# First attention of batches 0 and 1: the reciprocals of the row sums move from VectorE to PoolE, as a power of minus one

## The chip, the cores and the metric

The kernel runs on one core of a Trainium2 chip. The metric is the device time of one execution in microseconds (us). A core has five engines, each of which takes its own instructions in the order in which they were written: TensorE (PE, matmuls and transposes), VectorE (DVE), ScalarE (ACT), PoolE (POOL, the GpSimd engine) and SyncE (SP, which here issues DMAs). Engines wait for each other through semaphores.

## The reference

Two transformer layers over x of shape (8, 1024, 256). What the change touches is the first attention, done for each of the 8 batches:

```python
def _L0_attn_ref(x, Mq, Mk, Mv):
    q = (x @ Mq).reshape(B, H, C, K)          # B=8, H=8, C=1024, K=64
    k = (x @ Mk).reshape(B, H, C, K)
    v = (x @ Mv).reshape(B, H, C, V)          # V=32
    scores = jnp.einsum('bhqk,bhck->bhqc', q, k).reshape(B * H, C, C)
    att = jax.nn.softmax(scores / jnp.sqrt(jnp.float32(K)), axis=1)
    out = jnp.einsum('bqhc,bhcd->bqhd', att.reshape(B, C, H, C), v)
    return out.reshape(B, C, H * V)
x = x + _L0_attn_ref(_layernorm(x), Mq, Mk, Mv)
x = x + _L0_ffn_ref(_layernorm(x), ...)       # weights and rows quantised to FP4 blocks
x = x + _L1_attn_ref(_layernorm(x), ...)      # 16 heads of 16, q and k normalised
x = x + _L1_ffn_ref(_layernorm(x), ...)       # top 2 of 8 low-rank experts
```

The kernel divides by the softmax's row sum not in the 1024 x 1024 matrix of weights but in the rows of v that those weights multiply.

## The kernel before

The batches run through a pipeline written out by hand. Each stage of a batch is a lane: a generator for each engine that yields a place before each piece of work. The function `weave` merges an engine's lanes by these places (table `PLACES`), so an engine's order is fixed when the kernel is built and nothing moves at run time. While batch b is in its second attention and experts, batch b + 1 is in its first attention. At the start this overlap is missing: beside the first attention of batch 0 runs only the preparation of the weights (quantising them to FP4: lanes `prep` and `prep_weights`), then comes the first half of batch 0's FFN input alone, and the first attention of batch 1 runs beside the FFN of batch 0 and then beside the head normalisation of batch 0's second attention (`heads`, `heads_norm`).

The first attention of a batch has 64 steps n, each of 128 query rows against 1024 keys (step n is head group n // 8, block n % 8). A step is a chain over four engines:

- PE, `attn0`: scores of the step into one of two halves of PSUM tile `pS` (line 761), which it may write when the exponential of step n - 2 has read it (wait on `e0_in`).
- DVE, `attn0`: the negative row maximum (`nmaxa`, line 1635).
- ACT, `attn0`: exp into one of four buffers (`EA[n % 4]`, line 1274, three of them parts of region `ua`), with the row sum into a column of `zz`; it signals `e0_in`. It may write a buffer when the values of step n - 4 have been multiplied (`pv0_in`).
- DVE, `sums0`: the reciprocal of that column, 128x1, into `rz` (line 1644), signal `rz_in`.
- POOL, `attn0`: 256 columns of v times the reciprocal into one of four buffers `vs` (line 2160, also a part of `ua`), signal `vs_in`; the profile puts its wait on line 2159.
- PE, `values0`: vs times the exponentials, into PSUM tile `pV` (line 886). PE's lane puts the values of step n - 3 behind the scores of step n. After 8 steps ACT (in batches 0 and 1) copies `pV` to `oTa` and PE transposes it.

Beside this, DVE, ACT and POOL work on the other lanes. Those that matter below: POOL's `prep_weights` (lines 2350, 2353, 2356, 2358, 2366, in turns with DVE's `prep`, lines 2012 to 2026), POOL's part of the FFN's quantisation in batch 0 (lines 2204, 2206, 2211, 2212, between DVE's lines 1562 and 1572), and POOL's `heads` and `heads_norm` (lines 2258, 2266, 2276 to 2300). POOL already uses the power elsewhere: four lanes take (variance + eps) to the power -0.5 of 2, 4 or 8 columns (lines 2136, 2146, 2182, 2328), with the exponent in a 128x1 tile `half` that a memset has filled.

The two pieces that the change is about are these:

```python
c = n % 8                                                      # DVE, sums0
e.wait_ge(e0_in, 64 * b + n + 1)
e.reciprocal(rz[:, c:c + 1], zz[:, c:c + 1]).then_inc(rz_in, 1)

e.wait_ge(rz_in, 64 * b + m + 1)                               # POOL, attn0
e.tensor_tensor(vs[m % 4], vv[:, :, 32 * c:32 * c + 32],
                rz[:, c:c + 1].unsqueeze(2).to_broadcast([128, 8, 32]), ALU.mult).then_inc(vs_in, 1)
```

Of the kernel before, what the change touches and what calls it, by code (L numbers as in the profile page):

```python
# [7 lines left out]
F32 = mybir.dt.float32  # L8
# [3 lines left out]
ALU = mybir.AluOpType  # L12
# [338 lines left out]
def timed(engine):  # L351

    def of(lane):

        def at(*args):
            keys = [(engine, lane.__name__, *args[:n]) for n in range(len(args), -1, -1)]
            places = next((PLACES[k] for k in keys if k in PLACES), ())
            for _, place in zip(lane(*args), places, strict=True):
                yield place
        return at  # L360
    return of
# [14 lines left out]
def build(nc, a, out):  # L376
    with ExitStack() as ctx:

        def sb(name, shape, dt=F32):
            return ctx.enter_context(nc.sbuf_tensor(name, shape, dt))  # L380

        def sem(name):
            return ctx.enter_context(nc.semaphore(name))
# [89 lines left out]
        tqw = [ub(2816 * i, [FI]) for i in range(8)]  # L473
        scw = [[ub(48 * K + 512 * i + 176 * n, [44]) for n in range(2)] for i in range(2)]
        amw = sb("amw", [128, 44])
        raw = {"mq": ub(24 * K, [2, 512]), "mk": ub(28 * K, [2, 512]), "mv": ub(32 * K, [2, 256])}
        xhb = sb("xhb", [128, NT * D])
        xhb_flat = xhb[:, :]
# [23 lines left out]
        zz = sb("zz", [128, 8])  # L502
        rz = sb("rz", [128, 8])
# [23 lines left out]
        s0_in, max0_in, e0_in, rz_in, vs_in, pv0_in = (sem(n) for n in ("s0", "max0", "e0", "rz", "vs", "pv0"))  # L527
# [79 lines left out]
        def job_to(n, k, w):  # L607
            _, n0, rn, _, s_ = jobs[n]
            return wd[0:w, :, k, n0:n0 + 128] if s_ is None else wgu[:, :, k, s_, n0:n0 + rn]
# [128 lines left out]
        def _(e):  # L738
# [430 lines left out]
            @timed("PE")  # L1169
            def prep():  # L1170
                for n, (_, _, rn, cols, _) in enumerate(jobs):
                    yield
                    e.wait_ge(wq_in, 5 * n + 5)
                    for c0 in range(0, cols, 128):
                        w = min(128, cols - c0)
                        u = take(("w", n, c0))
                        i = transpose(bank(u)[0:w, 0:rn], tqw[4 * (n % 2) + 1][0:rn, c0:c0 + w])
                        if w < 128:
                            i = e.matmul(bank(u)[w:2 * w, 0:rn], tqw[4 * (n % 2) + 1][0:rn, c0:c0 + w], ident[0:rn, 0:rn])
                        i.then_inc(r_full[u.bank], 1)  # L1180
                yield
                for o in range(2):
                    e.wait_ge(wrow[o], 16 * 8)
                    for k in range(2):
                        u = take(("W", o, k))
                        transpose(bank(u)[:, 0:128], tqw[4 * o][:, k * 128:k * 128 + 128]).then_inc(r_full[u.bank], 1)
                yield
                e.wait_ge(raw1_in, 16 * 13)
                for k in range(2):
                    u = take(("A", k))  # L1190
                    transpose(bank(u)[:, 0:128], small[:, k * 128:k * 128 + 128])
                    transpose(bank(u)[:, 128:136], small[0:8, 256 + k * 128:384 + k * 128]).then_inc(r_full[u.bank], 1)
                yield
                e.wait_ge(wrow[0], 16 * (8 + 16))
                for o in range(2):
                    u = take(("B", o))
                    transpose(bank(u)[:, 0:128], tqw[0][:, 256 * o:256 * o + 128]).then_inc(r_full[u.bank], 1)
# [14 lines left out]
        def _(e):  # L1212
# [243 lines left out]
            @timed("ACT")  # L1456
            def prep():
                for n, (_, _, rn, cols, _) in enumerate(jobs):
                    yield
                    for c0 in range(0, cols, 128):  # L1460
                        high(("w", n, c0), job_to(n, c0 // 128, 128)[:, 0, :], WS, lambda v: v[:, 0:rn])
                yield
                for o in range(2):
                    for k in range(2):
                        high(("W", o, k), wmoe[:, 0, k, 128 * o:128 * o + 128], WS, lambda v: v[:, 0:128])
                yield
                for k in range(2):
                    u = full(("A", k))
                    e.activation(wmoe[:, 0, k, 264:392], bank(u)[:, 0:128], ACT.Copy, scale=WS)
                    e.activation(wmoe[:, 0, k, 256:264], bank(u)[:, 128:136], ACT.Copy, scale=WS).then_inc(r_mid[u.bank], 1)  # L1470
                yield
                for o in range(2):
                    high(("B", o), bt[:, 0, o * 128:(o + 1) * 128], WS, lambda v: v[:, 0:128])
# [22 lines left out]
        def _(e):  # L1496
# [141 lines left out]
            @timed("DVE")  # L1638
            def sums0(b):
                for n in range(64):  # L1640
                    yield
                    c = n % 8
                    e.wait_ge(e0_in, 64 * b + n + 1)
                    e.reciprocal(rz[:, c:c + 1], zz[:, c:c + 1]).then_inc(rz_in, 1)  # L1644

            @timed("DVE")
            def outputs0(b):
# [456 lines left out]
            def lanes_y(i):  # L2104
                return [*([first(i + 1, attn0), first(i + 1, sums0), first(i + 1, outputs0), first(i + 1, projections)] if within(i + 1) else []),
                        *([placed(-6, prep()), placed(-6, prep_low()), prep_heads()] if i < 0 else []),
                        *([v for lane in (moe_x3, moe_gate, moe_M) for v in second(i - 1, lane)] if within(i - 1) else []),
                        *([heads(i), heads_bias(i), heads_norm(i)] if within(i) and i + 1 < NB else
                          [heads_end(), heads_bias(i), heads_norm_end(), heads_by_end(), heads_low_end()] if i + 1 == NB else [])]
# [5 lines left out]
        def _(e):  # L2115
# [3 lines left out]
            e.affine_select(out=ident[:, :], in_=ident[:, :], compare_op=ALU.not_equal, fill=1.0, base=0,  # L2119
                            pattern=[[-1, 128]], channel_multiplier=1).then_inc(const_in, 1)  # L2120
            e.memset(halfp[:, :], 0.5).then_inc(const_in, 1)
            for n in range(8):
                e.memset(iota[:, n:n + 1], float(n)).then_inc(const_in, 1)
            e.memset(vaug[:, :, :, 16:17], 1.0 / AS).then_inc(const_in, 1)
# [23 lines left out]
            @timed("POOL")  # L2148
            def attn0(b):

                for m in range(64):
                    yield
                    c = m % 8
                    if m > 3:
                        e.wait_ge(pv0_in, 64 * b + m - 3)
                    if m == 0:
                        u = ring["v0", b, 3]
                        e.wait_ge(r_free[u.bank], u.n)
                    e.wait_ge(rz_in, 64 * b + m + 1)
                    e.tensor_tensor(vs[m % 4], vv[:, :, 32 * c:32 * c + 32], rz[:, c:c + 1].unsqueeze(2).to_broadcast([128, 8, 32]), ALU.mult).then_inc(vs_in, 1)  # L2160

# [216 lines left out]
            def lanes_y(i):  # L2378
                return [*([first(i + 1, attn0)] if within(i + 1) else []), *([placed(-6, prep()), placed(-6, prep_weights())] if i < 0 else []), *([v for lane in (moe_rstd, moe_low, moe) for v in second(i - 1, lane)] if within(i - 1) else []),
                        *([spread("H", i), heads(i), heads_norm(i)] if within(i) and i + 1 < NB else  # L2380
                          [spread("H", i), heads_end()] if i + 1 == NB else [])]
# [349 lines left out]
```

## Time and profile before

| | |
|---|---|
| median of 3 runs | 2743.35 us (2740.52 to 2746.29) |
| the profiled execution, its own time | 2740.36 us |
| its span in the profile | 2738.6 us |
| busy share of the span | PE 93%, DVE 74%, ACT 73%, POOL 44% |
| chain that ended last, by engine | PE 47%, DVE 20%, ACT 9%, DMA 8%, POOL 6%, issue 6%, SP's queue 4% |
| first attention of batch 0 | 37 to 211 us |
| first attention of batch 1 | 259 to 470 us |

The page gives averages over the whole span. The first 470 us, which the change touches, look different from the rest: the pipeline is filling, and the busy share of PE is lower there. So the views below are taken by stretches. The 1.8 us between the span and the execution's own time lie around the profiled instructions and are not touched.

### The profile page before, as it was taken

To read this page: it belongs to the slowest core of one execution; us is meant where nothing else is said; L and a number is where in the kernel's file an instruction comes from. 1 tells how busy PE (TensorE), PEld (TensorE's weight loads), DVE (VectorE), ACT (ScalarE), POOL (GpSimd) and SP (SyncE) were. 2 spreads that over 40 slices of the span, in tenths; PEclk is the share of its full clock that TensorE was granted. 3 is DMA by queue.
4 is the path that set the end of the run, shared out by engine and by line. 5 is a ranking of instruction groups with operands and counts; after the bars stand their busy time and mean duration, and the time that the engine had idled before them with its cause. 6 is when DMAs were issued, how large, how long until landed. Compare 5 with 4: busy or idle time off the path is not lost.

```text
span 2738.6 us, 115342 instructions
## 1 busy us (share of the span) xinstructions
PE 2550.1 (93%) x50126; PEld 1409.9 (51%) x50126; DVE 2033.8 (74%) x4228; ACT 1990.4 (73%) x3791; POOL 1213.8 (44%) x1744
## 2 busy tenths in 40 slices
PE   7776877999999999999999999999999999999898
PEld 4445644445644566445654466445664457443434
DVE  6778866957888589866888589875888678865534
ACT  4552556886778867887778867887778867787785
POOL 5564475216733268124752167223762267411210
PEclk9998999999999999999999999999999999999999
DMA  5214332325423362324423243324532254232310
GB/s 134 45 36 89 53 68 73 73 36 103 104 53 82 56 122 73 76 51 85 109 72 77 51 98 92 81 48 66 114 93 66 42 97 96 57 72 44 95 26 24
DMA packets 458145, 200.66 MB, mean 73 GB/s; under 512 B 270110, under 2 KB 447622, under 8 KB 457614
## 3 DMA queue, kind: packets, MB, share of 16 engines
q1 hardware_dynamic: 455982, 192.15, 33.0%
q8 instruction: 412, 6.75, 1.0%
q10 hardware_dynamic: 1632, 0.79, 0.2%
q14 instruction: 119, 0.97, 0.1%
HBM read 46.48 MB, written 32.51 MB: 29 GB/s over the span
## 4 chain that ended last, share of the span: by engine, by line
PE 47%; DVE 20%; ACT 9%; DMA 8%; POOL 6%; issue 6%; SPq 4%; ACTq 0%; DVEq 0%; POOLq 0%
PE pR L761 18%; PE pV L1025 11%; PE pS L984 7%; DVE nmaxa L1635 6%; ACT ub L1332 6%; PE pS L761 5%; PE pV L886 3%; PE pR L771 2%; DMA xT<-ua 2%; SPq L2633 2%; DMA ua<-EA 1%; POOL ua L2160 1%; DMA ua<-ua 1%; DMA xT<-xhb 1%; POOL ub L2300 1%
## 5 line engine op out<-in xcount | busy, mean ns | idle before, releaser
L1332 ACT ACTIVATE ub<-pS 128x512 f32<-128x512 f32 x2048 | 1048.7, 609 | 162.5 <-PE pS L984 160.6
L1635 DVE TENSOR_REDUCE nmaxa<-pS 128x1 f32<-128x1024 f32 x512 | 621.0, 1216 | 150.9 <-PE pS L761 148.7
L1274 ACT ACTIVATE ua<-pS,nmaxa 128x1024 f32<-128x1024 f32 x384 | 427.9, 1115 | 246.4 <-DVE nmaxa L1635 241.1
L761 PE MATMUL pS<-ua 128*32 128x512 f16 x8192 | 542.9, 386 | 61.4 <-ACT ua L1274 33.8
L1025 PE MATMUL pV<-ub,vaug 128*17 128x512 f32 x4096 | 537.7, 597 | 0.0
L2160 POOL TENSOR_TENSOR ua<-ua,rz 128x256 f32<-128x256 f32 x512 | 330.6, 659 | 284.7 <-DVE rz L1644 278.1
L984 PE MATMUL pS<-ub 50*128 50x512 f16 x1920 | 339.0, 383 | 8.6 <-ACT ub L1332 1.6
L761 PEld LDWEIGHTS pS<-ua 128*32 128x32 f16 x8192 | 209.0, 98 | 225.4 <-ACT ua L1274 54.2
L761 PE MATMUL pR<-wgu,xT 128*32 128x352 f16 x6144 | 283.2, 317 | 26.4 <-DVE ub L1701 14.1
L984 PEld LDWEIGHTS pS<-ub 50*128 50x128 f16 x1920 | 94.5, 93 | 365.3 <-ACT ub L1332 314.5
L886 PE MATMUL pV<-ua 128*32 128x128 f32 x6144 | 241.2, 278 | 29.5 <-POOL ua L2160 27.0
L761 PEld LDWEIGHTS pR<-wgu,xT 128*32 128x32 f16 x6144 | 158.8, 97 | 168.4 <-issue 107.8
L886 PEld LDWEIGHTS pV<-ua 128*32 128x32 f32 x6144 | 167.7, 111 | 99.4 <-POOL ua L2160 50.4
L1274 ACT ACTIVATE EA<-pS,nmaxa 128x1024 f32<-128x1024 f32 x128 | 142.6, 1114 | 76.2 <-DVE nmaxa L1635 75.5
L2211 POOL TENSOR_TENSOR EA<-ua,EA 128x64 f16<-128x64 f32 x28 | 8.6, 307 | 394.7 <-DVE EA L1753 394.7
L761 PE MATMUL pR<-wqkv,xT 128*32 128x512 f16 (+1 forms) x3072 | 146.0, 327 | 4.2 <-DMA xT<-xhb 1.5
L1025 PEld LDWEIGHTS pV<-ub,vaug 128*17 128x17 f32 x4096 | 88.1, 96 | 91.8 <-issue 71.3
L761 PE MATMUL pR<-wd,ua 128*32 128x256 f16 x3808 | 128.3, 273 | 5.7 <-DMA ua<-EA 5.6
L761 PEld LDWEIGHTS pR<-wd,ua 128*32 128x32 f16 x3808 | 97.0, 96 | 65.3 <-issue 63.9
L1223 ACT ACTIVATE ua<-pR 128x512 f16<-128x512 f32 x128 | 75.8, 601 | 69.8 <-PE pR L761 51.2
L2211 POOL TENSOR_TENSOR ua<-ua 128x64 f16<-128x64 f32 x28 | 8.7, 309 | 235.3 <-DVE ua L1753 235.3
L761 PEld LDWEIGHTS pR<-wqkv,xT 128*32 128x32 f16 x3072 | 83.4, 97 | 53.2 <-issue 3.4
(274 smaller groups left out, 4081.2 us busy)
## 6 DMA issues: line engine op xcount, KB each, us to landing
ua<-ua SPq DMA_DIRECT2D x378, 128.0 KB, 2.8
ub<-scr SPq DMA_DIRECT2D x264, 64.0 KB, 2.7
scr<-ub SPq DMA_DIRECT2D x30, 512.0 KB, 4.2
x<-in_L_attn_x SPq DMA_DIRECT2D x32, 256.0 KB, 4.0
between<-x SPq DMA_DIRECT2D x28, 256.0 KB, 3.3
ub<-between SPq DMA_DIRECT2D x28, 256.0 KB, 3.8
out<-ub SPq DMA_DIRECT2D x28, 256.0 KB, 3.4
ub<-scr SPq DMA_DIRECT2D x192, 32.0 KB, 1.8
```

Source lines behind the costliest of these rows:

```text
L761: i = e.matmul(dst[j:j + 32], w[:, j:j + 32], m, start=start, stop=stop)
L771: return e.matmul(dst, src, ident[0:n, 0:n], is_transpose=True)
L886: i = e.matmul(pV[32 * jl:32 * jl + 32, 128 * jg:128 * jg + 128], vs[n % 4][:, j, :], EA[n % 4][:, 128 * j:128 * j + 128], start=(c == 0 a ...
L984: e.matmul(pS[:, 512 * hl:512 * hl + 512], kk_[row:row + 50, o, 128 * c:128 * c + 128], q[row:row + 50, o, 512 * qh:512 * qh + 512]).then_ ...
L1025: i = e.matmul(pV[32 * hl:32 * hl + 17, :], vaug[:, c, 4 * hg + hl, :], EB[(4 * n + hl) % 8], start=(c == 0), stop=(c == 7))
L1223: e.activation(dst, view(bank(u)), ACT.Copy, scale=scale).then_inc(r_mid[u.bank], 1)
L1274: e.activation(EA[n % 4], pS[:, 1024 * (n % 2):1024 * (n % 2) + 1024], ACT.Exp, bias=nmaxa[:, n % 32:n % 32 + 1], accum_out=zz[:, n % 8:n ...
L1332: e.activation(EB[(4 * n + hl) % 8], pS[:, 512 * hl:512 * hl + 512], ACT.Exp).then_inc(e1_in, 1)
L1635: e.tensor_reduce(nmaxa[:, n % 32:n % 32 + 1], pS[:, 1024 * (n % 2):1024 * (n % 2) + 1024], AXX, ALU.max, negate=True).then_inc(max0_in, 1)
L2160: e.tensor_tensor(vs[m % 4], vv[:, :, 32 * c:32 * c + 32], rz[:, c:c + 1].unsqueeze(2).to_broadcast([128, 8, 32]), ALU.mult).then_inc(vs_i ...
L2300: e.tensor_tensor(hl[:, w_, 1, :, :], f, hl[:, w_, 0, :, :], ALU.subtract).then_inc(lo1_in, 1)
L2633: e.dma_start(dst[at:at + 16, o:o + 2, :], scr[b % 2, w_, l, 64 * hg:64 * hg + 64, :].rearrange("(h p d) n -> p d h n", p=2, d=16)[par]).t ...
```

## The change

For batches 0 and 1 the reciprocal leaves DVE. PoolE, ahead of its multiplication of a step, waits for the exponential itself and takes zz to the power of a tile that holds -1, into the same column of rz. It then waits for its own `rz_in` signal, as it waited for DVE's. Batches 2 to 7 are as before. One memset at the start fills the exponent. The places of all lanes stay.

```diff
+        minus = sb("minus", [128, 1], F32)
...
                 for n in range(64):
                     yield
                     c = n % 8
-                    e.wait_ge(e0_in, 64 * b + n + 1)
-                    e.reciprocal(rz[:, c:c + 1], zz[:, c:c + 1]).then_inc(rz_in, 1)
+                    if b > 1:
+                        e.wait_ge(e0_in, 64 * b + n + 1)
+                        e.reciprocal(rz[:, c:c + 1], zz[:, c:c + 1]).then_inc(rz_in, 1)
...
+            e.memset(minus[:, :], -1.0)
...
                     if m == 0:
                         u = ring["v0", b, 3]
                         e.wait_ge(r_free[u.bank], u.n)
+                    if b < 2:
+                        e.wait_ge(e0_in, 64 * b + m + 1)
+                        e.tensor_tensor(rz[:, c:c + 1], zz[:, c:c + 1], minus[:, 0:1], ALU.pow).then_inc(rz_in, 1)
                     e.wait_ge(rz_in, 64 * b + m + 1)
```

## Rows read from the trace of the kernel before

**Rows 1.** Windows: stretch, its length, busy us of each engine (instructions), PE clock, DMA
```profile
37.00:211.00 174.00, 127.71 (x2564) 75.62 (x2564) 134.42 (x298) 95.58 (x194) 101.07 (x130) 0.94 0.22 51
...
259.00:365.00 106.00, 93.84 (x2542) 67.91 (x2538) 92.26 (x169) 53.69 (x95) 49.31 (x56) 1.00 0.37 63
365.00:445.00 80.00, 59.49 (x1170) 34.93 (x1166) 49.24 (x82) 46.92 (x81) 65.63 (x114) 0.94 0.34 85
...
480.00:2400.00 1920.00, 1867.85 (x37800) 1036.28 (x37792) 1503.06 (x3076) 1500.88 (x2852) 885.92 (x1289) 1.00 0.37 78
```

**Rows 2.** Waits, 37 to 211 us: who waited for whom, us in total, times, longest
```profile
POOL ua L2160 <- DVE rz L1644: 60.7, 23, 10.1
...
PE pV L886 <- POOL ua L2160: 17.7, 18, 3.1
...
DVE rz L1644 <- ACT ua L1274: 10.0, 9, 2.2
```

**Rows 3.** The same view, 259 to 365 us
```profile
POOL ua L2160 <- DVE rz L1644: 39.8, 13, 7.0
```

**Rows 4.** The same view, 365 to 466 us
```profile
POOL ua L2160 <- DVE rz L1644: 10.8, 7, 3.1
...
PE pV L886 <- POOL ua L2160: 10.1, 8, 4.4
```

**Rows 5.** Lines 1644 and 2160 up to 466 us: count, ns min/median/max, first and last start
```profile
L1644 DVE RECIPROCAL rz<-zz x128: 132/153/639, 38.7 to 465.0; 128x1 f32<-128x1 f32 x128
...
L2160 POOL TENSOR_TENSOR ua<-ua,rz x128: 603/614/1265, 39.0 to 465.3; 128x256 f32<-128x256 f32 x128
```

**Rows 6.** POOL's powers by form, whole span: count, busy us, mean ns, idle before
```profile
L2182 POOL TENSOR_TENSOR rstdF<-varF,half 128x4 f32<-128x4 f32 x16 | 16.6, 1039 | 1.3
...
L2146 POOL TENSOR_TENSOR rstdH<-varH,half 128x8 f32<-128x8 f32 x8 | 13.3, 1664 | 0.7
```

**Rows 7.** Timeline, start of the kernel: start, length, engine, line, idle before
```profile
4.57 0.23 POOL L2134 TENSOR_SCALAR var<-ag 128x2 f32<-128x2 f32 x1 [1.61 <-DVE ag L1527]
4.87 0.72 POOL L2136 TENSOR_TENSOR rstd<-var,half 128x2 f32<-128x2 f32 x1
...
7.39 1.87 POOL L2136 TENSOR_TENSOR rstd<-var,half 128x2 f32<-128x2 f32 x1
7.47 1.22 DVE L1584 SCALAR_TENSOR_TENSOR mq<-ub,mq 128x1024 f16<-128x1024 f32 x1
```

**Rows 8.** Timeline, last two steps of batch 0's first attention
```profile
203.48 1.11 ACT L1274 ACTIVATE ua<-pS,nmaxa 128x1024 f32<-128x1024 f32 x1
...
205.81 1.11 ACT L1274 ACTIVATE EA<-pS,nmaxa 128x1024 f32<-128x1024 f32 x1 [1.13 <-DVE nmaxa L1635]
...
207.85 1.19 POOL L2160 TENSOR_TENSOR ua<-ua,rz 128x256 f32<-128x256 f32 x2 [3.54 <-DVE rz L1644]
...
208.52 1.08 PE L886 MATMUL pV<-ua 128*32 128x128 f32 x16 [3.14 <-POOL ua L2160]
```

**Rows 9.** Timeline, a reciprocal that DVE waits for between two maxima
```profile
166.95 1.05 PE L761 MATMUL pS<-ua 128*32 128x512 f16 x16 [0.32 <-ACT ua L1274]
...
168.74 0.17 DVE L1644 RECIPROCAL rz<-zz 128x1 f32<-128x1 f32 x1 [1.14 <-ACT ua L1274]
168.82 1.21 DVE L1635 TENSOR_REDUCE nmaxa<-pS 128x1 f32<-128x1024 f32 x1
```

**Rows 10.** Timeline of POOL, weight preparation: multiplications in a full queue
```profile
155.65 1.75 POOL L2160 TENSOR_TENSOR ua<-ua,rz 128x256 f32<-128x256 f32 x3
```

**Rows 11.** Timeline of POOL, head normalisation of batch 0
```profile
373.64 0.61 POOL L2160 TENSOR_TENSOR ua<-ua,rz 128x256 f32<-128x256 f32 x1 [1.25 <-DVE rz L1644]
...
398.50 0.61 POOL L2160 TENSOR_TENSOR ua<-ua,rz 128x256 f32<-128x256 f32 x1 [3.14 <-DVE rz L1644]
...
409.20 2.33 POOL L2160 TENSOR_TENSOR ua<-ua,rz 128x256 f32<-128x256 f32 x4
413.32 1.17 POOL L2300 TENSOR_TENSOR ub<-ub 128x512 f16<-128x512 f32 x1 [1.79 <-ACT ub L1428]
```

**Rows 12.** Chain that ended last, 410 to 475 us: start, length, what
```profile
443.35 1.16 POOL ub L2300
```

## The prediction

> **What bounds the kernel now.** I read the busy time by stretches first [rows 1]. From 480 to 2400 us PE is busy 1867.85 of 1920 us (97%): it bounds the kernel there, and nothing of the change lies there. Earlier it doesn't: 127.71 of 174 us (73%) in batch 0's first attention, 93.84 of 106 (89%) while batch 1's runs beside batch 0's FFN, 59.49 of 80 (74%) beside the head normalisation. Since the later work is a full PE queue, a shift of the moment at which PE fills up goes through to the end one for one. So the question is only how much earlier or later PE gets there.
>
> In the early stretches no engine is full (DVE 77, 87, 62%; POOL 58, 47, 82%): what binds is the hand-over between queues. The waits show it: in batch 0's attention POOL stands 60.7 us in front of its multiplication for DVE's reciprocal, in 23 waits, and PE then 17.7 us for POOL [rows 2]. Beside the FFN of batch 0 it is 39.8 us [rows 3], beside the head normalisation 10.8 us, with PE 10.1 us behind POOL [rows 4]. A wait "for the reciprocal" begins, though, before the exponential has ended; only the part behind that is DVE's lateness.
>
> **What the change removes.** 128 reciprocals, median 0.153 us [rows 5]. Back to back with other work each takes less of the DVE queue than its length, since starts overlap the instruction before by some 0.1 us: I count 0.08 us each, 64 x 0.08 = 5.1 us in batch 0's attention and 2.6 us in each half of batch 1's. About half of it lies where DVE's queue leads the chain: -2.5, -1 and -0.5 us.
>
> It also removes DVE's waits for the exponential in front of a reciprocal, 10.0 us in batch 0's attention [rows 2]. They cost only where the next DVE work was ready. Where it was [rows 9], the scores for the next maximum ended at 168.00, DVE was held by the reciprocal until 168.82, so 0.8 us come free. In most others the next work had itself to wait, or ACT or PE was not ready to use it. I take -2 us for batch 0 and -1 us in each half of batch 1.
>
> Third, it removes DVE's lateness for POOL. The clearest case is the end of the stretch [rows 8]: the exponential of step 62 ended at 204.59, but its reciprocal stood behind two long DVE instructions, POOL began at 207.85 and PE stood idle for 3.14 us. With the change POOL can have it at 204.6 + 0.2 + 0.63 = 205.4. Step 63, whose exponential ends at 206.92, then decides: multiplied by 206.92 + 0.2 + 0.63 + 0.61 = 208.4, and with one value product of 0.65 us PE is done at 209.0, not at 210.46 (the second product began at 209.38 and took 1.08). That is -1.5 us, and the chain goes through here. In other places PE's idle time ahead of such a product is 0.1 to 1.4 us; I take -1 us for all of them in batch 0 and -0.5 in batch 1's first half.
>
> **What it adds.** 128 powers of one column on POOL. No row has one column. Two columns took 0.72 us undisturbed [rows 7], four 1.04, eight 1.66 [rows 6]: 0.16 us a column, so 0.72 - 0.16 = 0.56 us for one. Ends: 0.40 (no column at all, same line) and 0.72 (no less than two). I take 0.55, nearest to the line. POOL's wait for its own signal adds a gap, 4.87 - 4.80 = 0.07 us [rows 7]. So 0.63 us a step on POOL's queue, 40 us in batch 0's attention and 20 in each half of batch 1's. What is queued behind: the multiplication, for which PE waits, and then the weight preparation, the FFN's rounding or the head normalisation. Against it stands POOL's own wait: where it stood for a late reciprocal, the power fits in. Step by step, the shorter of POOL's wait and of the time from exponential to multiplication (less 0.1) sums to 52 us over batch 0's 64 steps (out of 60.7 [rows 2]), more than the 40 added; to 31 (of 39.8 [rows 3]) against 20 beside the FFN; but to 10.5 (of 10.8 [rows 4]) against 20 beside the head normalisation. The cost is where POOL's queue is full.
>
> - Batch 0: three multiplications at 155.65 stand in such a queue [rows 10], with five more up to 171 us; 5 of these 8 lie on the chain, +3 us. The first steps, for which POOL and PE already wait, add +1 us.
> - Batch 1, beside the FFN: one multiplication stood between DVE's late reciprocal and line 2204 on the chain at 265 us and now runs 4 us earlier; -0.5 us net with the powers that fall behind 2206.
> - Batch 1, beside the head normalisation: POOL is busy 65.63 of 80 us [rows 1], and 20 powers are added. I followed its queue [rows 11]. The wait of 1.25 us at 373.64 pays for two powers. Five steps (385 to 394 us) add 3.2 us. The wait of 3.14 us at 398.50 takes that back but for 0.7. One more step makes 1.4 us; the four of 409.20 add 2.5, of which the 1.79 us in front of line 2300 (which itself shifts by 1.4) takes back nearly 2; then one step more. At 423 us POOL is late by about 2.8 us, and another block of four adds a little through PE. The chain leaves this stretch by POOL's line 2300 [rows 12], by a DMA and SP: +4 us.
>
> The memset (0.1 us) lies in a start in which POOL waits for DVE 1.61 us [rows 7]: nothing, and 0.1 us without that cover. No DMA and nothing of SP or ACT moves place.
>
> A rule speaks against the change. In the rows a power costs four times the reciprocal (0.55 against 0.153 us). The Trainium skill ("GPSIMD Engine Reference", section 3) calls GpSimd the wrong choice for elementwise work, with VectorE about twice as fast. By length alone the sum would be 128 x 0.4 = 51 us slower; by the rows it isn't, since engine time is not what binds here.
>
> A second thing can lengthen a power: that of 7.39 took 1.87 us in place of 0.72, and DVE's line 1584, which reads two SBUF tensors, ran 1.22 us within it [rows 7]. In the first 466 us the multiplications met this twice in 128 (median 614, longest 1265 ns) [rows 5], so for 128 powers 1 us or less; I take 0.5. The skill names it too (same page, section 8: shared SBUF interfaces, contention with VectorE's two-input instructions), and the trace agrees.
>
> **Sum.** Batch 0: -2.5 - 2 - 1.5 - 1 + 3 + 1 = -3. Batch 1 beside the FFN: -1 - 1 - 0.5 - 0.5 = -3. Beside the head normalisation: -0.5 - 1 + 4 = +2.5. Contention +0.5, and +1 for the ring of four exponential buffers, which a later value product holds longer. Together -2 us: the profiled execution's 2740.36 becomes 2738.4. It stood 3 us below the median of the runs, so by the median 2743.35 becomes 2741.3.
>
> **The rivals.**
> - The hand-over was the bound (faster). If the early stretches are one loop of queues holding each other, taking DVE out of it gives back most of PE's waits for POOL, 17.7 + 10.1 us [rows 2, 4], not the few that I credit. For it: waits of up to 10.1 us for an instruction of 0.153. Against it: PE would often wait next for a maximum or an exponential. Half of 27.8 us, less the 4 already counted, is -10 more: -12 us, 2731; the near edge is -6.
> - POOL becomes the bound (slower). In the head normalisation 65.63 + 20 x 0.63 = 78.2 of 80 us: full. If POOL's waits there (1.79, 3.14) don't shrink because their releasers are delayed with it, 20 us of powers less 4.4 us of late reciprocals cost +15 rather than +4, and the crowded preparation near 155 us gives +3 more. It decides once POOL's share in 365 to 445 us passes 95%. Net with my other terms: -2 + 11 + 3 = +12, 2755; the near edge is +6.
> - The power is dearer than the line says: at 0.72 us a step costs 0.16 more, about 20 steps in full queues, +3 us: 2744. At 1.3 us (twice the two-column row; the exponent -1 on sums up to 1024 has no row) it would be +14: 2755.
> - The change does nothing: then 2743.4, as the forecast, within the measure.
>
> **Chances.** The forecast's case (-5.4 to +5.4 us) 0.38, with the plain nothing in it; hand-over 0.36; POOL bound 0.20; power dearer than 1 us 0.06. What this kernel's measurement tells from no change is about 0.2%, 5.5 us. So faster 0.36, same 0.38, slower 0.26. The likeliest case's own range is 2738 to 2747; 8 in 10 asks for the near parts of both rivals: 2730 to 2753.
>
> **What would show it.** Right: the reciprocal's line with 384 instructions in place of 512; 128 powers near 0.55 us; POOL's busy time up by 70 us; its wait ahead of each step now on ACT and in total under half of 111 us; PE's first full stretch beginning 2 us earlier; batch 0's attention ending near 208, the second half of batch 1's having lost some of it. Wrong on the faster side: PE's waits for POOL down by ten or more in batch 0. Wrong on the slower side: POOL over 95% busy in 365 to 445 us and line 2300's last run of that stretch more than 5 us later than the attention of batch 0 alone would put it. A power of over 0.8 us would make the whole sum wrong.

## The result and the profile after

The changed kernel is slower: median 2757.35 us against 2743.24 us of the kernel before, run beside it (five runs each); ratio 1.0045, 95% interval 1.0031 to 1.0059. One of its five runs took 3591.66 us, at a granted clock of 0.65 in place of 0.98, and isn't in the ratio. The profiled execution took 2755.29 us against 2740.36 us before: +15 us, where I had forecast -2. The time is close to that of the rival "POOL becomes the bound" (2755).

In the changed kernel the numbers of POOL's lines are 6 higher than in the kernel before (its multiplication is line 2166, the power before it 2164; what was line 2300 is 2306), those of PE and ACT and most of DVE's 1 higher. The kernels of the study differ by another line or two.

The busy time by stretches of the changed kernel (to compare with [rows 1]; columns: stretch, length, then PE, weight load, DVE, ACT and POOL busy with their counts, granted clock, DMA share, GB/s):

```profile
37.00:211.00 174.00, 126.07 (x2558) 75.68 (x2546) 128.51 (x225) 95.04 (x195) 134.62 (x191) 0.93 0.23 51
259.00:365.00 106.00, 93.50 (x2494) 67.55 (x2498) 89.73 (x136) 51.84 (x94) 67.16 (x86) 0.98 0.35 62
365.00:445.00 80.00, 57.23 (x1166) 34.07 (x1158) 44.79 (x57) 44.13 (x77) 71.15 (x127) 0.94 0.35 87
445.00:480.00 35.00, 23.60 (x428) 13.62 (x431) 22.93 (x28) 17.51 (x32) 28.86 (x39) 0.90 0.26 64
480.00:2400.00 1920.00, 1866.37 (x37742) 1036.28 (x37738) 1494.82 (x3067) 1499.13 (x2850) 883.54 (x1288) 1.00 0.37 77
```

Behind 480 us next to nothing has changed. Beside the head normalisation POOL is up from 65.63 to 71.15 of 80 us, and PE has done 2.3 us less. The fourth line is a stretch that [rows 1] leave out, though the attention reaches into it: there POOL is busy 28.86 of 35 us, and was 14.08 before. Part of that is work that only comes later, since the windows stand still and the kernel is 12 us late by then.

```profile
445.00:480.00 35.00, 27.12 (x484) 13.00 (x476) 23.41 (x45) 23.35 (x45) 14.08 (x15) 1.00 0.25 61
```

The two lines of the step, up to 480 us (count, busy us, mean ns, idle before and its releasers), to compare with [rows 5], and then two of the waits of 369 to 480 us (total, times, longest), to compare with [rows 4]:

```profile
L2166 POOL TENSOR_TENSOR ua<-ua,rz 128x256 f32<-128x256 f32 x128 | 81.2, 634 | 10.0
L2164 POOL TENSOR_TENSOR rz<-zz,minus 128x1 f32<-128x1 f32 x128 | 73.3, 573 | 35.7 <-ACT ua L1275 29.3 <-ACT EA L1275 5.3 <-PE pV L887 0.9
```

```profile
DVE nmaxa L1636 <- PE pS L762: 32.8, 18, 5.6
...
PE pV L887 <- POOL ua L2166: 14.1, 7, 5.0
```

The power costs what I took (median 548 ns). POOL's idle time ahead of a step is down to 35.7 us, and what is left of it is a wait for the exponential. PE waits longer for POOL than before (14.1 us against 10.1 [rows 4]), and DVE waits 32.8 us for PE's scores, 15.1 in the kernel before: VectorE has room, which nobody fills.

To see where the time is lost, I take the end of the same value product in two traces, both from their span's start. The changed kernel is late by 2.0 us at step 9 of batch 0, early by 2.1 at step 40, late by 4.1 at step 46, by 3.4 at the end of batch 0's attention (step 63) and by 3.6 at step 94 (the last beside the FFN; steps 64 and up are batch 1's). Then it is 5.9 (step 99), 8.5 (105), 8.4 (110, at 426 us of the kernel before), 10.8 (115), 12.3 (121), and 12.5 us when PE's queue fills up at 480 us. So 9 of the 12.5 us are lost beside the head normalisation and the input of batch 1's FFN.

### The profile page after: what moved, and what is told of

Same layout as the page of the kernel before. It is cut to its first block, busy times and chain, and to the rows that moved or that the text cites. A ratio compares the mean times of both kernels' runs of the same rounds, so it can differ in the third digit from the quotient of the medians.

```text
span 2753.5 us, 115343 instructions
## 1 busy us (share of the span) xinstructions
PE 2554.3 (93%) x50126; PEld 1416.2 (51%) x50126; DVE 2027.1 (74%) x4100; ACT 1988.9 (72%) x3791; POOL 1286.0 (47%) x1873
## 4 chain that ended last, share of the span: by engine, by line
PE 47%; DVE 18%; POOL 9%; ACT 9%; DMA 7%; issue 5%; SPq 4%; ACTq 0%; DVEq 0%; POOLq 0%
PE pR L762 18%; PE pV L1026 11%; PE pS L985 7%; ACT ub L1333 6%; PE pS L762 5%; DVE nmaxa L1636 5%; PE pV L887 3%; PE pR L772 2%; DMA xT<-ua 2%; POOL ua L2166 2%; DMA ua<-EA 2%; SPq L713 1%; SPq L2639 1%; POOL rz L2164 1%; DMA xT<-xhb 1%
## 5 line engine op out<-in xcount | busy, mean ns | idle before, releaser
L762 PE MATMUL pR<-wgu,xT 128*32 128x352 f16 x6144 | 285.2, 319 | 25.9 <-DVE ub L1703 11.8
```

Source lines behind the costliest of these rows:

```text
L762: i = e.matmul(dst[j:j + 32], w[:, j:j + 32], m, start=start, stop=stop)
```

## The experiments

The study has a base of its own, in which SP's transposing copies from SBUF to SBUF are plain ones of the same size, so what the matmuls behind them compute differs. The expectation below puts the first of these copies at 472 us. That is wrong: in the trace before, 15 of the 140 start earlier, the first at 211.2 us, so all of batch 1's attention has some beside it. That the base serves is therefore a matter of measurement (below). All shifts are of value products against this base's trace (q0), in us. Since PE is full behind 480 us, the shift of step 127 is what counts; by the last value product, at some 2345 us, it has moved on by -3 to +7 us.

```diff
-    e.dma_start(half_of(xT, hf), half_of(pairs, hf), transpose=True)
+    e.dma_start(half_of(xT, hf), half_of(pairs, hf).rearrange("p (n c) -> p n c", c=128))
```

(and the same for the copies of the FFN's hidden rows; the diffs of the study are excerpts, and all kernels in it have the plain copies.)

> The kernel before, with one thing left out: the sixteen-bit transposition of the copies from SBUF to SBUF that SP starts (inputs of the FFN, the MoE and the heads). They copy the same bytes to the same place untransposed, so what the matmuls behind them compute differs, not how long they take. This is the base of the other kernels of the study. Expected by every theory: the first 460 us as in the kernel before (no such copy is needed before 472 us), the whole somewhere within 3% of it, as far as a plain copy takes another time than a transposing one.

> The changed kernel with the same plain copies: it must be slower than the base by 8 to 16 us, with the PE's shift at 465 us after the start between +11 and +14 us, or the study of the cause can't be made on this base.

The base: 2724.78 us, ratio to the kernel before 0.9927; steps 1 to 8 of the two traces agree with a steady -0.4 us, and against the kernel before the base is at +0.3 at step 63, +0.8 at step 94 and +0.7 at step 127. The median matmul of line 761 takes 273 ns in both. The changed kernel on it: 2734.50 us, ratio 0.9959 (0.9946 to 0.9972), so 0.3% above the base's 0.9927 (0.9911 to 0.9942); shift at step 127 +12.1 (the changed kernel with its transposing copies: +11.8 against the same base). The base serves.

**Powers without relief, relief without powers.**

```diff
 # q2: DVE keeps its reciprocals
+    e.tensor_tensor(spare[:, c:c + 1], zz[:, c:c + 1], minus[:, 0:1], ALU.pow).then_inc(spare_in, 1)
+    e.wait_ge(spare_in, 64 * b + m + 1)
     e.wait_ge(rz_in, 64 * b + m + 1)
 # q3: no reciprocal at all
-    e.tensor_tensor(rz[:, c:c + 1], zz[:, c:c + 1], minus[:, 0:1], ALU.pow).then_inc(rz_in, 1)
-    e.wait_ge(rz_in, 64 * b + m + 1)
+    e.wait_ge(e0_in, 64 * b + m + 1)
-    e.tensor_tensor(vs[m % 4], vv[:, :, 32 * c:32 * c + 32], rz[:, c:c + 1].unsqueeze(2).to_broadcast([128, 8, 32]), ALU.mult)
+    e.tensor_tensor(vs[m % 4], vv[:, :, 32 * c:32 * c + 32], zz[:, c:c + 1].unsqueeze(2).to_broadcast([128, 8, 32]), ALU.mult)
```

> Plain copies; POOL takes its 128 powers as in the changed kernel, into a tile that nobody reads, and waits for each before it multiplies; VectorE keeps its 128 reciprocals and POOL waits for those too. It has the cost of the powers without the relief of VectorE. Theory Q (the powers cost where POOL's queue is full, above all beside the head normalisation, and VectorE's relief is worth 2 to 4 us): +15 us against the base, that is 2 to 4 above the changed kernel. Rival D (VectorE's relief is worth the 9 us that I predicted in batch 0 and beside the FFN, and the powers cost over 20): +21 us or more. Rival W (the powers cost nothing, it is the order in which VectorE and ScalarE now run): at most +3 us.

> Plain copies; the first attention of batches 0 and 1 takes no reciprocal at all: POOL waits for ScalarE's row sum itself and multiplies by it (so what is computed differs there). It has VectorE's relief and none of the powers. Theory Q: -3 us against the base (-1 to -5), most of it in batch 0. Rival D: -9 us or better. Rival W: as slow as the changed kernel, +10 or more.

Measured: both 2749.96 us (ratio 1.0020), none 2711.74 us (0.9877). The shifts, with those of later kernels:

```
step (us in base)   q1 changed  q2 both  q3 none  r3 cheap  s4 wide  s3 pairs
9    (64.5)            +2.9      +8.1     +0.7     +1.7      +7.5     +4.3
63  (210.8)            +3.5     +14.2     -6.3     -5.1     +23.8     +7.8
94  (367.0)            +1.7     +14.0     -8.4     -7.0     +25.2    +11.8
127 (470.0)           +12.1     +24.7     -9.9     -3.7     +46.3    +28.7
```

Each column is one execution, and kernels that are the same program up to a step show how far it can be trusted. At step 63 the base's program stands at -0.3, 0, -0.5 and -3.3 (kernel before, q0, r2, s1), the changed one's at +3.0, +3.5, +7.0 and +5.6 (changed kernel, q1, r1, s2). From step 94 to 127 they agree better: +0.1, 0, +0.7 and -0.4 with reciprocals on VectorE (kernel before, q0, r1, r4), +9.0, +10.4 and +11.5 with powers (changed kernel, q1, r2). So the loss beside the head normalisation is well above the scatter; in batch 0 single shifts are good to 3 or 4 us.

Theory Q's figures fall, Rival D's hold: relief is worth 9.9 us (q3), or 24.7 - 12.1 = 12.6 (q2 less q1), and the powers cost 12.1 + 9.9 = 22 us, or 24.7. Of q2's 24.7 us some are its start: its first maximum began at 35.43 us against 33.33 in the base, before any power. By part (batch 0, beside the FFN, beside the head normalisation), relief gives -6.3, -2.1, -1.5 by q3 and -10.7, -1.6, -0.3 by q1 less q2, and the powers (q1 less q3) cost 9.8, 0.3 and 11.9. I had formed theory Q after the result, with a relief of 2 to 4 us; my blind sum had been nearer. The order of work on the other engines (Rival W) costs nothing: q3 has it too and is faster than the base.

In q3 the line of the multiplication shows what room the step has by itself when nothing stands before it:

```profile
L2166 POOL TENSOR_TENSOR ua<-ua,zz 128x256 f32<-128x256 f32 x128 | 79.3, 635 | 66.7 <-ACT ua L1275 49.3 <-ACT EA L1275 12.1 <-PE pV L887 5.0
```

The base has 112.6 us there, nearly all put down to DVE's reciprocal. Without reciprocals 66.7 us of idle time are left: over half of the "room" was a wait for the exponential.

**One part alone.** Each is the changed kernel with the condition on batch and step cut, for both engines.

```diff
-    if b < 2:                       # POOL takes the power, else DVE the reciprocal
+    if b < 1:                       # r1
+    if b == 1 and m > 30:           # r2
+    if b == 0 and 8 < m < 42 or b == 1 and m < 31:    # r4
```

> Plain copies; only batch 0's first attention is changed, batch 1's is as before (DVE takes those reciprocals). From the traces of q0, q1 and q3 (base, changed, no reciprocals; shift of the PE against the base at the end of batch 0: +3.5 with powers, -6.3 with nothing). Theory Q (a power costs where it stands in POOL's queue, and the parts add up): +3.5 at 211 us and still +3 to +4 at 480 us, total +3 to +5 us against the base. Rival L (lateness from batch 0 grows in batch 1, since POOL gets to the head normalisation late): +6 or more at 480 us. Rival N (batch 1's cover takes it back): under +1.5.

> Plain copies; POOL takes the powers only in steps 31 to 63 of batch 1, beside the heads' normalisation; all others stay DVE's. Theory Q: the PE is at +10 (+9 to +11) at 480 us, the total +10 to +12 against the base: these 33 powers are nearly the whole loss. Rival L: as POOL comes into this part on time, only half of it, +5. Rival S (128 equal shares of the loss of 22 us that q1 and q3 show, less DVE's relief): 33 shares are 5.9, less 1.5: +4.4.

> Plain copies; POOL takes the powers only where q1's trace went ahead of the base: steps 9 to 41 of batch 0 and steps 0 to 30 of batch 1 (64 powers); DVE keeps the other 64 reciprocals. Shifts of q1 against the base: +2.9 to -1.7 over the first stretch, +3.5 to +1.7 over the second. Theory Q: -4.6 - 1.8 = -6 us against the base (-3 to -8). Rival T (the gain is time borrowed: POOL's backlog from step 41 meets DVE's hand-over at 155 us and gives it back): -1 to +2.

```
step         r1 batch 0   r2 heads half   r4 chosen steps
0               +2.2          +0.6             +3.0
9               +5.1          +0.7             +3.9
40              +1.1          -1.3             +0.0
44              +6.5          -0.5             +4.8
63              +7.0          -0.5             +2.7
94              +6.9          -0.7             +2.4
127             +7.6         +10.8             +2.0
total, ratio  2731.35, 0.9933  2735.17, 0.9949  2727.13, 0.9913
```

r2 is the plainest result: these 33 powers alone cost 10.8 + 0.7 = 11.5 us (theory Q: +10; an equal share of all powers: +4.4). They don't need batch 0's lateness, so Rival L falls. The whole times are coarser than this. By the ratios r2 is 6 us above the base, r1 1.6 us above and r4 3.8 below, and all three intervals overlap the base's (r1 0.9917 to 0.9949, r2 0.9934 to 0.9964, r4 0.9899 to 0.9928). The base's trace is of a run of 2720.13 us where the median is 2724.78, which may put all shifts against it some us too high; a difference between two steps of one column is free of that. r1 carries its 7.0 us through batch 1 and is at 7.6 in the end: lateness is handed on, not absorbed and hardly grown (Rival N falls too, by the trace). It was expected at +3.5: 5.1 us were there by step 9, against 2.9 in q1, the same program up to there. In r4 the first nine steps are as in the base, and yet it is 3.0 us late at step 0: arrival of the first loads scatters by about that much, and of the first steps' shift in q1, r1 and s4 I can't say how much is due to powers.

r4 shows no gain from a choice of steps: it gains 3.9 us from step 9 to 40 and loses 4.8 us by step 44, where it takes no power. Rival T (borrowed time) holds: -1.0 us from step 0 to 127, where I expected -6.

**Cheaper and dearer.** The same waits and as many instructions, another duration.

```diff
-    e.tensor_tensor(rz[:, c:c + 1], zz[:, c:c + 1], minus[:, 0:1], ALU.pow)
+    e.tensor_tensor(rz[:, c:c + 1], zz[:, c:c + 1], minus[:, 0:1], ALU.mult)                # r3
+    e.tensor_tensor(wide[:, 4 * c:4 * c + 4], zz[:, c:c + 1].to_broadcast([128, 4]),
+                    minus[:, 0:1].to_broadcast([128, 4]), ALU.pow)                          # s4
```

> Plain copies; the changed kernel with POOL's power replaced by a product of the same one-column operands (the row sum by minus one), which leaves the reciprocal out; same order, same waits, same number of instructions. No row shows a product of 128x1 on POOL; of 128x64 it takes 0.32 us. Taking 0.1 to 0.2 us for it against 0.55: Theory D (the time of the powers in the queue is what costs): of the 22 us between q1 and q3 a share of (0.15 + 0.07) / 0.62, 8 us: -2 us against the base (-5 to +1). Rival I (what costs is the added wait and instruction, whatever it does): +10, as the changed kernel.

> Plain copies; the changed kernel with each power over four equal columns, of which one is used (rows: 1.04 us for 128x4 against 0.55 for one column): 133 us of powers against 73.6, everything else and what is computed the same. Theory D with an even price of 0.33 for each us: +12 + 0.33 x 60 = +32 at 480 us. If instead POOL is the bound from here on wherever the powers stand, each us costs nearly one: +60. Rival I (the number of instructions and waits decides, not their time): +12.

(s4's multiplication reads the first of the four columns.) The line of each up to 480 us; s4 is so late that 13 of its 128 powers start behind 480 us, the last at 511.7, and all 128 sum to 133 us:

```profile
L2164 POOL TENSOR_TENSOR rz<-zz,minus 128x1 f32<-128x1 f32 x128 | 25.7, 200 | 52.7 <-ACT ua L1275 40.5 <-ACT EA L1275 9.7 <-PE pV L887 2.2
```

```profile
L2165 POOL TENSOR_TENSOR wide<-zz,minus 128x4 f32<-128x4 f32 x115 | 118.3, 1029 | 21.9 <-ACT ua L1276 20.7 <-ACT EA L1276 1.0
```

Measured 2723.85 us (0.9905) and 2767.49 us (1.0080). At step 127 that is -3.7, +12.1 and +46.3 for 25.7, 73.6 and 133 us of it: 0.33 us for each of the first 48 us, 0.57 for each of the next 60 (I expected +32 with an even price). So duration decides, not the added instruction and wait alone (Rival I), and the price depends on the place. The instruction and its wait aren't free either: r3, with a product of 0.20 us, is 6.2 us behind q3, which has none. Beside the FFN (steps 63 to 94) the three differ by only -1.9, -1.8 and +1.4; beside the head normalisation (94 to 127) they move +3.3, +10.4 and +21.1: there 34 powers longer by 0.36 us cost 7.1 of 12.2 us, and longer by another 0.46 us 10.7 of 15.6. Each us put into POOL there costs 0.6 to 0.7.

**Room for POOL.** Both with less other work for POOL beside the head normalisation.

```diff
-    e.tensor_tensor(xb, xb, bproj[:, :], ALU.add)
+    e.tensor_tensor(xb[:, 0:k], xb[:, 0:k], bproj[:, 0:k], ALU.add)              # k = 32 in batch 0
-    e.tensor_tensor(qg, qg, y[:, 32 * t:32 * t + 32].unsqueeze(2).to_broadcast([128, 32, 16]), ALU.mult)
+    e.tensor_tensor(qg[:, :, 0:k], qg[:, :, 0:k], y[:, 32 * t:32 * t + 32].unsqueeze(2).to_broadcast([128, 32, k]), ALU.mult)   # k = 2
```

> Plain copies; the base (DVE takes all reciprocals) with less work for POOL beside batch 1's second half: the eight additions of the projection's bias in batch 0 reach 32 columns in place of 256, and the eight products by the norm reach 2 of each 16 columns, so that part is left out. By the rows (0.79 and 1.06 us each for the whole) POOL has some 12 us less to do between 375 and 445 us. Expected: 0 to -3 us at 480 us against the base (POOL had idle time there, and the base waits for POOL only in places).

> Plain copies; the changed kernel with the same work left out as in s1. What counts is how far it falls behind s1 between step 94 (367 us) and 480 us; without the omission that was +10.4 (q1 against q0) and +11.5 (r2 against q0). Theory Q (the powers cost what does not fit in POOL's queue): with 12 us of room more, +1 to +4. Rival C (each power lengthens the step's chain by its 0.6 us, full queue or not): +9 or more, as before.

2715.51 us (0.9901) and 2723.38 us (0.9919). The stretches of 365 to 445 us of q0, q1, s1 and s2, in this order:

```profile
365.00:445.00 80.00, 60.68 (x1178) 35.53 (x1174) 49.17 (x83) 46.48 (x82) 65.85 (x117) 0.91 0.31 87
```

```profile
365.00:445.00 80.00, 58.20 (x1128) 33.93 (x1120) 44.22 (x55) 42.37 (x75) 70.24 (x125) 0.89 0.31 87
```

```profile
365.00:445.00 80.00, 63.12 (x1226) 36.83 (x1230) 53.10 (x89) 50.60 (x88) 57.99 (x116) 0.91 0.29 86
```

```profile
365.00:445.00 80.00, 61.06 (x1222) 36.29 (x1218) 47.08 (x59) 47.24 (x82) 67.16 (x137) 0.94 0.32 88
```

The work left out is 9.9 us (additions 6.0 to 2.2 us, products 8.4 to 2.3). From step 94 to 127 the powers' kernel lost 4.7 - 3.1 = 1.6 us in place of 10.4: room for POOL takes back 8.8 of them. But the base, too, gained 5.7 us (-4.0 to -9.7), where I expected 0 to 3: POOL's queue already set the pace there before the change. The gap between the two is still 7.3 us, between the +1 to +4 of theory Q and the +9 of Rival C. A queue at 82% (65.85 of 80) was not one with room. And in s1, where POOL is busy 72% (57.99 of 80), the same powers still cost 7.3 in place of 10.4 us: a full queue is not all of it, and room in the sum is not room at the step. How the 7.3 us part between queue and step stays open; it is also the weakest figure here, since s1's trace is of a run 6 us below its median and s2's of one 10 us above, and by the medians the two whole kernels are 7.9 us apart (q0 and q1: 9.7).

**Two steps in one power.**

```diff
+    if b < 2 and m % 2 == 0:
+        e.wait_ge(e0_in, 64 * b + m + 2)
+        e.tensor_tensor(rz[:, c:c + 2], zz[:, c:c + 2], minus[:, 0:1].to_broadcast([128, 2]), ALU.pow).then_inc(rz_in, 1)
```

(both multiplications of the pair wait for this one signal.)

> Plain copies; the changed kernel with one power of two columns for two steps, taken when the second step's row sum is there: 64 powers of 0.72 us (46 us of POOL, against 73.6 in q1, 25.7 in r3, 0 in q3), computed in full. Theory D (between r3 at -3.7 and q1 at +12.1 at 480 us each us of powers costs 0.33): +3 at 480 us, better than the changed kernel and no better than the base. Rival E (the first step of each pair now waits for the exp of the second, some 1.3 to 2.9 us later, and PE waits for it): +12 or more, so no gain from the shorter queue.

2752.04 us (1.0026), +28.7 at step 127, the worst but for s4, although its powers take 47 us in place of 73.6 (64 x 0.732). The power's line up to 480 us, of q1 and of s3 (whose attention lasts until 499 us), with POOL's idle time before it, and then PE's waits for the multiplication in the same stretch:

```profile
L2164 POOL TENSOR_TENSOR rz<-zz,minus 128x1 f32<-128x1 f32 x128 | 73.6, 575 | 34.3 <-ACT ua L1275 28.9 <-ACT EA L1275 5.1
```

```profile
L2164 POOL TENSOR_TENSOR rz<-zz,minus 128x2 f32<-128x2 f32 x60 | 43.9, 732 | 91.6 <-ACT ua L1275 57.1 <-ACT EA L1275 26.9 <-PE pV L887 7.4
```

```profile
PE pV L887 <- POOL ua L2166: 37.4, 26, 5.0
```

```profile
PE pV L887 <- POOL ua L2166: 39.6, 31, 5.5
```

Rival E's figure holds, and by more than I gave it. POOL stands 91.6 us in front of its powers in place of 34.3, nearly all of it for exponentials, and what it saved in length doesn't come back: the delay until the second exponential costs more than 27 us of POOL's time are worth. PE's own waits for the multiplication show little of it (39.6 against 37.4 us). Both exist, then: the length of POOL's queue where it is full, and the time from exponential to multiplication.

## Why the prediction was wrong

Two steps failed: the cover that POOL's waits were to give the powers in batch 0 (+4 us stood for a cost of 9.8), and the working beside the head normalisation, which stopped at 423 us and let the chain leave POOL there (+4 for 11.9).

**What it removes: right in sum.** The terms for VectorE came to -7 in batch 0, -3 beside the FFN (0.5 of it net of powers) and -1.5 beside the head normalisation; relief alone (q3) measured -6.3, -2.1 and -1.5. The match part by part is closer than single traces allow: q1 less q2 gives -10.7, -1.6 and -0.3. The power's price was right too: 0.55 us and a gap of 0.07. The +1 us for the ring of exponential buffers was not measured by itself.

**Batch 0's queue, +4 against 9.8 measured (q1 less q3).** I let 5 of 8 crowded multiplications count and took the other powers as covered by POOL's waits, 52 us of cover for 40 us of work. The cover was counted from waits that the trace puts down to DVE's reciprocal, each by its length in the old schedule. It doesn't last: q3, with neither reciprocal nor power, keeps 66.7 of the 112.6 us as waits for the exponential, and where VectorE's relief brings scores and exponentials forward they meet POOL's other work. The timeline of POOL in the changed kernel shows the place of the largest single loss (start, length, line; then PE's product that waited for the first multiplication):

```profile
152.35 1.66 POOL L2362 TENSOR_TENSOR ub<-ub 128x704 f32<-128x704 f32 x1
154.10 1.67 POOL L2364 TENSOR_TENSOR ub<-ub 128x704 f32<-128x704 f32 x1
155.72 0.56 POOL L2164 TENSOR_TENSOR rz<-zz,minus 128x1 f32<-128x1 f32 x1
156.36 0.61 POOL L2166 TENSOR_TENSOR ua<-ua,rz 128x256 f32<-128x256 f32 x1
```

```profile
157.03 1.08 PE L887 MATMUL pV<-ua 128*32 128x128 f32 x16 [4.40 <-POOL ua L2166]
```

These are the multiplications of [rows 10]; they start no earlier than before (156.36 against 155.65), though value products were 2.1 us ahead two steps earlier. What relief had gained by then waits in front of POOL. r4 meets the same wall without a power in these steps (+0.0 at step 40, +4.8 at step 44), and even q3 loses 2.5 us there (-6.4 to -3.9).

**The last two steps of batch 0, -1.5 against +0.2 (+3.2 at step 61, +3.4 at step 63).** The shape was as foreseen: the power of step 62 needn't wait for VectorE. But VectorE's two-input line 1573 now starts 0.16 us ahead of it; before, the same instruction (line 1572) started at 205.70 us, 1.1 us behind the end of step 62's exponential. That VectorE's relief moved it isn't shown: in q2, which keeps the reciprocals, it also starts right behind that exponential, 0.11 us after the power has begun. The changed kernel:

```profile
209.01 1.81 POOL L2164 TENSOR_TENSOR rz<-zz,minus 128x1 f32<-128x1 f32 x1 [1.13 <-ACT ua L1275]
210.91 0.61 POOL L2166 TENSOR_TENSOR ua<-ua,rz 128x256 f32<-128x256 f32 x1
```

```profile
208.85 1.21 DVE L1573 SCALAR_TENSOR_TENSOR xhb<-xhb,scx 128x1024 f32<-128x1024 f32 x1
```

```profile
211.57 0.64 PE L887 MATMUL pV<-ua 128*32 128x128 f32 x16 [2.99 <-POOL ua L2166]
```

1.26 us more than the usual length, on the chain; PE stands idle for 2.99 us, nearly the 3.14 of [rows 8]. q1, r1 and s2 met the same at this step (1.82, 1.81 and 1.87 us). In all, four of the 128 powers were lengthened, by 2.8 us together; I had taken 0.5. The place is what mattered, and I had put both of these in separate terms.

**Beside the FFN, -3 against -1.8 (q1) and +0.2 (the changed kernel's own trace).** The powers cost nothing there (0.3), as said; the relief was 2.1, and traces of one program scatter by 2 us and more here.

**Beside the head normalisation, +2.5 against 9 (cost alone +4 against 11.9).** I followed POOL's queue up to 423 us and had it late by 2.8 us there. The waits of [rows 11] paid as I said: those of 3.14 and 1.79 us are gone from the changed kernel's timeline. My count of powers was short: [rows 1]'s stretch of 365 to 445 us holds 23 multiplications in the timeline of the kernel before, not 20. And the size was off: behind the twelve powers from 389 to 423 us the third normalisation starts at 424.11 us in place of 416.26, 7.85 us later, of which 3.6 came from before: 4.2. And then the step of the working failed altogether: I stopped there, and allowed 1.2 us for what follows. Fourteen more powers follow from 431 to 469 us, 14 x 0.62 = 8.7 us, and from step 110 to 127 the lateness grows by 4.0 (8.4 to 12.5). I had let the chain leave POOL with line 2300 at 443.35 us [rows 12] for a DMA. In the changed kernel it doesn't. The chain that ended last, in order of time (start, length, what; its L2300 is line 2294 of the kernel before, its L2195, L2198 and L2201 are 2189, 2192 and 2195):

```profile
446.22 2.08 POOL ub L2300 x2
...
460.44 2.35 POOL ua L2195
...
462.88 2.37 POOL xhb L2198
465.24 0.50 POOL rz L2164
...
465.82 1.23 POOL ua L2166
467.05 0.50 POOL rz L2164
...
467.63 1.15 POOL ua L2166
468.78 0.50 POOL rz L2164
...
469.36 0.61 POOL ua L2166
469.97 2.10 POOL ua L2201
472.07 0.02 issue
472.09 4.38 DMA xT<-ua
476.47 0.86 issue
477.33 1.08 PE pR L762 x24
```

The last normalisation, late, holds PE and through it VectorE until line 2195 can start at 460.44, where the kernel before had the same instruction at 449.65. Then three powers stand between POOL's lines 2198 and 2201, the input of batch 1's FFN, for which PE waits at 477.33. In the kernel before POOL was idle for 1.30 and 0.64 us there, and the last of the three instructions started at 458.19 us in place of 469.93. The stretch ends by another chain than the one that I had read.

**The rivals.** "POOL becomes the bound" had the time, and its cause is the main one. One of its two signs came: line 2300's last run of the stretch starts at 454.13 us (as line 2306) against 443.35, 7.4 us more than batch 0's 3.4. The other, over 95% of POOL in 365 to 445 us, did not (89%, 71.15 of 80), because a busy share doesn't measure a queue: between small instructions that follow each other at once the profile leaves gaps of some 0.08 us, and they count as idle. From 375 to 456 us the changed kernel's POOL is busy 72.81 of 81 us (90%), and yet its timeline has only these two waits:

```profile
404.79 1.16 POOL L2306 TENSOR_TENSOR ub<-ub 128x512 f16<-128x512 f32 x1 [1.11 <-ACT ub L1429]
406.12 1.16 POOL L2306 TENSOR_TENSOR ub<-ub 128x512 f16<-128x512 f32 x1 [0.17 <-ACT ub L1429]
```

It stood still for 1.3 us in 81: the queue was full. The chain that ended last lies on POOL for 57 of these 81 us, 36 in the kernel before. The kernel before had 14.4 us of "idle" POOL in 365 to 445 us, of which only 8.6 were waits (1.25, 3.14, 1.79, 1.77, 0.50 and 0.16 us); 23 powers of 0.63 us are 14.5. That the powers don't fit could be read before the run. "The hand-over was the bound" was half right: relief alone does give 10 us, but there is no relief without a price on POOL. "The power is dearer" fell. What stays open is how much of the 2.0 us at the first nine steps is the powers' doing and how much is scatter of the first loads. A version in which the reciprocal leaves VectorE without 0.6 us on POOL was not found: the chosen steps (r4) match the base within the measure, and pairs (s3) are slower. How the cost in batch 0, 9.8 us with a scatter of 3 to 4, spreads over its steps is shown for the largest loss alone.

## What to carry to other kernels

A wait in a trace is room only if its releaser doesn't also move: when work goes from engine A to engine B, ask how much of B's wait in front of the step would be left without A's work (in q3, 66.7 of 112.6 us: waits for the exponential, which a power has to wait for as well), and expect A's gain to arrive at B's queue. Read a queue's room from its waits, not from its busy share: here 82% left 8.6 us of waits in 80, and each us added cost 0.6 to 0.7, not nothing until 95%. And follow the loaded queue to the point where the full engine takes over, here PE at 480 us, not to the place where the old chain leaves it.

## What the runs showed of the hardware

- On POOL a product of one column takes 0.19 us (median, r3), a power of one 0.55 (q1), of two 0.70 (s3), of four 1.01 (s4): the power's price is in the columns as well as in the start.
- A power of one column that started 0.16 us behind VectorE's two-input line 1573 took 1.81 us, three times its length. In the changed kernel 4 of 128 were lengthened: three beside two-input instructions (1.81, 1.46 and 1.00 us) and one, of 0.77 us, beside a TENSOR_SCALAR. The Trainium skill ("GPSIMD Engine Reference", section 8) has this contention with VectorE's two-input instructions; the trace agrees, 1.81 against 0.55 us. In q2 the same power started 0.11 us ahead of that VectorE instruction and took 0.55 us: here the order of the two starts went with the length.
- With plain copies in place of transposing ones the program is 0.73% faster (ratio 0.9927), about 20 us for the 140 of them, even though PE is busy at 97% for most of the time. From issue to landing the copies of line 2426 took 4.6 us transposing and 3.3 us plain (medians), those of line 2447 3.5 and 2.5 us.
